# Constant ones for the warm-up, halves of W's first pieces on two engines, and V's and W's blocks in one load per step

## What is computed

```python
base = x @ W.T                                  # W 1024 x 1024
gates = top-2 softmax(x @ Wr.T + 5 * onehot(ids))
h = base + 2.0 * einsum('bter,bte,eor->bto', x @ A, gates, B)   # 8 experts, rank 16
hits = softmax(h @ cent.T / 0.1) > 0.01         # 64 clusters
query_sel, cluster_sel = hits.any(1), hits.any(0)
dense = h @ V.T + bias
out = x + where(query_sel & cluster_sel[assignments], dense, 0)
```

## Time and profile before

| | us |
|---|---|
| time, median of 3 | 334.21 (334.06 to 334.86) |
| the profiled execution's own time | 334.7 |
| its span | 332.9 |
| TensorE busy | 328.9 (99%) |
| VectorE busy | 263.0 (79%) |
| ScalarE busy | 137.2 (41%) |

### The profile page before, as it was taken

The page is one execution under the profiler, slowest core; times in us unless marked ns, Lnnn a source line. Parts: engine busy times, 40 slices in busy tenths (PEclk is TensorE's granted clock), DMA queues, the critical chain, the costliest instruction groups (busy, mean ns, idle before and its releaser), DMA issues.

```text
span 332.9 us, 4578 instructions
## 1 busy us (share of the span) xinstructions
PE 328.9 (99%) x1748; PEld 287.3 (86%) x1748; DVE 263.0 (79%) x477; ACT 137.2 (41%) x231; POOL 1.0 (0%) x9
## 2 busy tenths in 40 slices
PE   8999999999999999999999999999999999999996
PEld 5888889999999999999877888888888888888886
DVE  4837967168988998989996979679398594997995
ACT  4824645245755664765633313232223331331310
POOL 1000000000000000000000000000000000000000
PEclk9999999999999999999999999999999999999999
DMA  7965600333524433335712371805508237060113
GB/s 248 417 192 224 248 2 1 126 129 126 185 97 132 158 128 126 128 105 184 282 43 85 119 259 77 294 9 196 185 1 289 89 130 250 0 234 20 63 66 126
DMA packets 14070, 48.05 MB, mean 144 GB/s; under 512 B 1696, under 2 KB 1952, under 8 KB 14048
## 3 DMA queue, kind: packets, MB, share of 16 engines
q1 hardware_dynamic: 14048, 47.75, 40.5%
HBM read 39.36 MB, written 8.39 MB: 143 GB/s over the span
## 4 chain that ended last, share of the span: by engine, by line
PE 99%; DVE 0%; issue 0%
PE ps L1061 26%; PE ps L1062 26%; PE ps L1063 26%; PE ps L1142 8%; PE ps L1070 7%; PE ps L1144 4%; PE ps L1067 1%; PE ps L1155 1%; PE ps L1162 0%; PE ps L1164 0%; PE ps L1219 0%; DVE nat L1054 0%; DVE warm L694 0%; PE ps L1213 0%
## 5 line engine op out<-in xcount | busy, mean ns | idle before, releaser
L1061 PE MATMUL ps<-vt_hi,w_hi 128*128 128x288 f32 (+1 forms) x184 | 58.7, 319 | 0.0
L1063 PE MATMUL ps<-vt_hi,w_lo 128*128 128x288 f32 (+1 forms) x184 | 58.0, 315 | 0.0
L1062 PE MATMUL ps<-vt_lo,w_hi 128*128 128x288 f32 (+1 forms) x184 | 58.0, 315 | 0.0
L429 ACT ACTIVATE u<-ps 128x512 f32<-128x512 f32 x31 | 18.5, 597 | 80.9 <-PE ps L1063 54.2
L1062 PE MATMUL ps<-gop_lo,sl_s_hi 128*128 128x512 f32 x128 | 49.8, 389 | 0.0
L1142 PE MATMUL ps<-aw,xt_hi 128*128 128x400 f32 x128 | 38.9, 365 | 0.0
L1061 PE MATMUL ps<-gop_hi_t,sl_s_hi 128*128 128x512 f32 x96 | 37.4, 390 | 0.0
L1063 PE MATMUL ps<-gop_hi_t,sl_s_lo 128*128 128x512 f32 x96 | 37.3, 389 | 0.0
L1062 PEld LDWEIGHTS ps<-vt_lo,w_hi 128*128 128x128 f32 x184 | 34.6, 188 | 1.6
L1061 PEld LDWEIGHTS ps<-vt_hi,w_hi 128*128 128x128 f32 x184 | 34.5, 188 | 1.6
L1063 PEld LDWEIGHTS ps<-vt_hi,w_lo 128*128 128x128 f32 x184 | 34.5, 188 | 1.5
(11 more groups left out here) (144 smaller groups left out, 657.9 us busy)
## 6 DMA issues: line engine op xcount, KB each, us to landing
xt_raw<-in_xt SPq DMA_DIRECT2D x32, 512.0 KB, 3.9
nat<-in_x SPq DMA_DIRECT2D x16, 512.0 KB, 4.1
out<-nat SPq DMA_DIRECT2D x15, 512.0 KB, 2.7
w_raw<-in_w SPq DMA_DIRECT2D x7, 512.0 KB, 3.3
wraw<-in_w SPq DMA_DIRECT2D x5, 512.0 KB, 4.7
vt_raw<-in_v SPq DMA_DIRECT2D x4, 576.0 KB, 5.0
vt_raw<-in_v SPq DMA_DIRECT2D x4, 256.0 KB, 4.7
wq_raw<-in_wq SPq DMA_DIRECT2D x4, 256.0 KB, 4.8
```

The costliest lines, as they stand in the source:

```text
L429: return nc.scalar.activation(dst, src, ACT.Copy)
L1061: nc.tensor.matmul(dst, l_hi, r_hi, start=start, stop=False, skip_group_check=True)
L1062: nc.tensor.matmul(dst, l_hi, r_lo, start=False, stop=False, skip_group_check=True)
L1063: return nc.tensor.matmul(dst, l_lo, r_hi, start=False, stop=stop, skip_group_check=True)
```

## The change

- WARM_UP goes from 9 to 18, each warm-up matmul has 256 columns instead of 512, and both its operands are the framework's constant 1.0 in bfloat16, read with a step of zero, which GpSimd writes before the kernel's own instructions. The zeroed tile, its memset and its semaphore are gone.
- V's and W's pieces lie in one tensor vw in HBM and in one tile vw_raw in SBUF (128 x 8 x 2 x 512). Step 0's two pieces are still loaded one by one; from step 1 on one load brings both, with rows of 4 KB (one block) or 8 KB (two blocks). The tile lies in space that G uses later, and the lo parts no longer take the place of the raw values.
- In the steps 0 and 1 DVE copies W's columns 0 to 255 and ACT columns 256 to 511. TensorE waits for V's hi part and DVE's half, and for ACT's half ahead of the third block. From step 2 on ACT copies the whole of W's piece.
- Step 0 goes through the same loops as the others.
- The two halves of hit_sum are added by DVE, and TensorE counts them in one matmul.

```diff
-WARM_UP = 9
+WARM_UP = 18
...
+                if p == 0:
+                    sp.dma_start(vw_raw[:, 0, 0, :], piece(0, 1)).then_inc(v0_landed, 16)
+                    sp.dma_start(vw_raw[:, 0, 1, :], piece(1, 2)).then_inc(wq0_landed, 16)
+                else:
+                    sp.dma_start(vw_raw[:, j0:j1, :, :].rearrange("p k h f -> p (k h f)"),
+                                 piece(2 * j0, 2 * j1)).then_inc(vw_landed[p - 1], 16)
...
-                act.wait_ge(v1_landed[p], 16)
-                copy(vt1_hi[:, j, :], vt1_raw[:, j, :]).then_inc(v1_hi, 1)
-                act.wait_ge(wq_landed[p], 16)
-                copy(wq_hi[:, j, :], wq_raw[:, j, :]).then_inc(wq_hi_done, 1)
+                act.wait_ge(v0_landed if p == 0 else vw_landed[p - 1], 16)
+                copy(vt1_hi[:, j, :], vw_raw[:, j, 0, :]).then_inc(v1_hi, 1)
+                if p == 0:
+                    act.wait_ge(wq0_landed, 16)
+                cols = slice(2 * P, HALF) if p <= 1 else slice(0, HALF)
+                copy(wq_hi[:, j, cols], vw_raw[:, j, 1, cols]).then_inc(wq_hi_done, 1)
...
+                if p <= 1:
+                    dve.wait_ge(wq0_landed if p == 0 else vw_landed[0], 16)
+                    nc.vector.tensor_copy(wq_hi[:, j, 0:2 * P], vw_raw[:, j, 1, 0:2 * P]).then_inc(wq_half_hi, 1)
                 dve.wait_ge(v1_hi, p + 1)
...
-            nc.vector.memset(warm[:], 0.0).then_inc(warm_ready, 1)
...
-            nc.vector.tensor_copy(hit_b[:], hit_sum[:]).then_inc(hit_ready, 1)
+            nc.vector.tensor_tensor(hit_b[:], hit_sum[:, 0, :], hit_sum[:, 1, :], ALU.add).then_inc(hit_ready, 1)
...
-            pe.wait_ge(warm_ready, 1)
+            ones = nc.const_aps.tensor(1.0, [P, QUARTER], BF16)
             for _ in range(WARM_UP):
-                nc.tensor.matmul(ps[:, 0, :], warm[:, 0:P], warm[:], start=True, stop=True)
+                nc.tensor.matmul(ps[:, 0, 0:QUARTER], ones[:, 0:P], ones, start=True, stop=True)
...
+            for p in range(len(STEPS) - 1):
                 js = range(*STEPS[p])
                 pe.wait_ge(v1_hi, p + 1)
-                pe.wait_ge(wq_hi_done, p)
+                pe.wait_ge(wq_half_hi, min(p, 1) + 1)
                 for m in range(NQ):
+                    if m == (2 if p <= 1 else 0):
+                        pe.wait_ge(wq_hi_done, p + 1)
                     for j in js:
-                        first(m, wq_hi, j, vt1_hi)
+                        first(m, wq_hi, j, vt1_hi, start=j == 0)
```

More of the change, by code:

```diff
@@ L57, with adaln_ffn_kernel @@
 BANK_X, BANK_Y, BANK_V, BANK_W = range(4)
-def adaln_ffn_kernel(nc, x, xt, ids, w9, wq, awt, v1, v2, bias, assign, out):
+def adaln_ffn_kernel(nc, x, xt, ids, w9, vw, awt, v2, bias, assign, out):
     x_t = x.rearrange("b s d -> (b s) d")
@@ L90, in adaln_ffn_kernel @@
         hit_sum = sb("hit_sum", [P, 2, C], F32)
[L91 removed]
+        hit_b = sb("hit_b", [P, C], BF16)
         csel = sb("csel", [C, P], BF16)
@@ L117, in adaln_ffn_kernel @@
         hgt_all = sb("hgt_all", [P, NT * P], F32)
-        with nc.sbuf_tensor("warm", [P, HALF], BF16) as warm:
+        with nc.sbuf_tensor("vw_raw", [P, KO, 2, HALF], F32) as vw_raw:
             pass
@@ L184, in adaln_ffn_kernel @@
         ps_hgt = ps[:, BANK_HGT, 0:2 * P]
-        wq_landed = [sem(f"wq_landed{p}") for p in range(len(STEPS))]
-        wq0_hi = sem("wq0_hi")
+        wq0_landed = sem("wq0_landed")
+        wq_half_hi = sem("wq_half_hi")
         wq_hi_done = sem("wq_hi_done")
         wq_split = sem("wq_split")
-        v1_landed = [sem(f"v1_landed{p}") for p in range(len(STEPS))]
+        v0_landed = sem("v0_landed")
+        vw_landed = [sem(f"vw_landed{p}") for p in range(1, len(STEPS))]
         v2_landed = [sem(f"v2_landed{p}") for p in range(PIECES)]
@@ L328, in load_first, with piece @@
                 j0, j1 = STEPS[p]
[L329 to L335, removed]
+                def piece(a, b):
+                    return vw[0, a * P * HALF:b * P * HALF].rearrange("(q f) -> q f", q=P)
+                if p == 0:
[4 more added lines that the diff above has]
+                                 piece(2 * j0, 2 * j1)).then_inc(vw_landed[p - 1], 16)
             def load_v2(p):
@@ L462, in t_part @@
                 copy(gop_hi_t[:, :, jj, :], gop_raw[:, T1:T4 + 1, jj, :]).then_inc(t_hi, 1)
-            act.wait_ge(v1_landed[0], 16)
-            copy(vt1_hi[:, 0, :], vt1_raw[:, 0, :]).then_inc(v1_hi, 1)
-            for p in range(1, len(STEPS)):
+            for p in range(len(STEPS)):
                 split_first(p)
@@ L1211, in hit_counts @@
                 pe.wait_ge(hit_ready, 1)
-                for c in range(2):
-                    last = nc.tensor.matmul(ps[0:C, 7, 0:P], hit_b[:, c, :], ones_b[:], start=(c == 0), stop=(c == 1))
-                last.then_inc(count_ready, 1)
+                nc.tensor.matmul(ps[0:C, 7, 0:P], hit_b[:], ones_b[:], start=True, stop=True).then_inc(count_ready, 1)
             def column_mask():
@@ L1338, in both @@
         return [V[lo:hi], V[HALF + lo:HALF + hi]]
-    def in_steps(a):
-        return np.concatenate([a[:, j0:j1].reshape(1, -1) for j0, j1 in STEPS], 1)
-    v1 = in_steps(turned(np.concatenate(both(0, A1) + [cent], 0)).transpose(1, 0, 2).reshape(P, KO, HALF))
+    v1 = turned(np.concatenate(both(0, A1) + [cent], 0)).transpose(1, 0, 2).reshape(P, KO, 1, HALF)
     v2 = turned(np.concatenate(both(A1, A1 + A2) + both(A1 + A2, HALF), 0))
     w9 = np.concatenate([b, w], 0)
-    wq = in_steps(w9[0:NQ].reshape(NQ, P, KO, P).transpose(1, 2, 0, 3).reshape(P, KO, NQ * P))
-    return {"xt": xt, "w9": w9, "wq": wq, "awt": awt, "v1": v1, "v2": v2}
+    wq = w9[0:NQ].reshape(NQ, P, KO, P).transpose(1, 2, 0, 3).reshape(P, KO, 1, HALF)
+    vw = np.concatenate([v1, wq], 2)
+    pieces = [vw[:, 0, 0], vw[:, 0, 1]] + [vw[:, j0:j1] for j0, j1 in STEPS[1:]]
+    vw = np.concatenate([a.reshape(1, -1) for a in pieces], 1)
+    return {"xt": xt, "w9": w9, "vw": vw, "awt": awt, "v2": v2}
 def kernel(**inputs):
```

26 lines of the change are left out of this document (8 added, 18 removed).

## The result

The changed kernel takes 335.53 us (334.35 to 335.99, 11 runs) against 334.58 us (334.06 to 334.86, 11 runs) for the kernel before: 1.0026 of it, 95% interval 1.0016 to 1.0036. It is slower by 0.26%, where the forecast was 333.85 and a gain. The size is within what the text called hard to tell from no change, but eleven runs tell it, and it has the other sign and lies outside the range.

A forecast was written before the change was run, and what follows sets the result against it. TensorE, busy 99% of 332.9 us, was taken as the bound. An earlier step 1 gave 0.22 us, with hit counts 0.36, so 334.21 became 333.85; the range ran from 333.3 less 0.1 to 334.6.

The forecast's parts named there:

- Part 1, the warm-up: At the kernel's start, TensorE begins warm-up at about 0.80 us instead of 1.18, 0.38 earlier, without a wait.
- Part 2, the halves: W's step 0 copy split: DVE's half takes 0.29 us, ACT's 0.40; TensorE's first load at 4.52, 0.14 sooner.
- Part 3, one load per step: From step 1 on, V and W land together; step 1's weights are ready at 7.50 us instead of 7.72.
- The gate: Earliest start of TensorE's step 1 matmuls by its bytes: landing plus 0.95 us for wait, copy, semaphore and weights load.
- L: Landing time of step 1's double load, bounded by 6.14 and 6.77 us and taken as 6.55.
- the 8.2 which the forecast named as a sign of being wrong: Start of TensorE's step 1, expected at 7.4 to 7.7 or about 8.0 us; past 8.2 the forecast is wrong.
- Rival 4: Step 1's double piece lands late, at 7.4, so TensorE starts it at 8.35, 0.6 us worse: 334.7; chance 0.06.
- The sentence on coalescing: Skill's rule to join small transfers into one large; by it step 1 lands at or below 6.14, never gating.
- Part 4, hit counts: Near 173 us, one small TensorE matmul fewer saves 0.14 us (0.05 to 0.21); DVE's add costs nothing.
- The sum: Whole kernel, median run: 0.22 us from step 1's earlier start, with hit counts 0.36, giving 333.85 from 334.21.
- Rival 3: Hole of up to 0.2 us after warm-up makes TensorE's clock rise late, at 9.5 us: 336.3; chance 0.04.
- the median run as one in which the clock was up when the real work began: At TensorE's first real matmul, the median run of 334.21 us is assumed to pay no half-rate stretch, costing 0.45.

The follow-up runs named there:

- the two-load kernel: Changed kernel with V's and W's pieces of steps 1 to 3 loaded separately, steps 4 and 5 still double: 334.37 us against 334.44, ratio 0.9996.
- the trace with 7.69: Changed kernel, double loads kept, step 2's load held until V's step 0 piece landed, W's halves at step 0 alone: 334.35 us against 334.61, ratio 0.9992.
- the changed kernel's second trace: Changed kernel, nothing altered, measured once more in a later group against the kernel before: 335.13 us against 334.48, ratio 1.0014.
- held loads: Changed kernel, SyncE issuing step 2's load only once V's step 0 piece has landed: 334.60 us against 334.65, ratio 0.9999.
- The joint wait: Changed kernel with steps 1 to 3 in two loads, ScalarE and VectorE waiting for both pieces before copying either: ratio 0.9998 to the kernel before.
- the fastest kernel: Changed kernel with steps 1 to 3 in two loads and W's halves at step 0 alone: 334.14 us, ratio 0.9991; again 334.05, ratio 0.9984.

## Why the prediction was wrong

**Part 1, the warm-up: right.** TensorE's first instruction came at 0.77 (0.73 to 0.85 forecast), no wait is left. Alone it shortened the span by 0.26, of a size that its interval doesn't tell from nothing.

**Part 2, the halves: right in size.** 0.29 and 0.42 us against 0.29 and 0.40. The first real load began at 4.65, not 4.52, because W's step 0 piece landed at 4.24 in this execution and 4.12 in the other; counted from the landing it is 0.41 against 0.54 before. At step 1 the halves are not needed with two loads: without them the two-load kernel has a span of 332.41 and 332.34, with before's at 332.79 and 332.86. With double loads they are, as the trace with 7.69 shows.

**Part 3, one load per step: the step that failed.** The gate was L + 0.95, and that held to 0.14 us or better: in the changed kernel's second trace the copy starts at 7.44, the weights load at 8.12, and the first matmul takes the array at 8.23 by the spacings, and at 8.12 + 0.19 = 8.31 at the latest, against 7.42 + 0.95 = 8.37. That is past the 8.2 which the forecast named as a sign of being wrong. What failed is the bound on L, "by 6.14 (V's bytes alone) and 6.77 (both)". It was read off one execution of single loads, as if bytes in the same order landed at the same time however they are cut, and in every execution. Double loads with 4 KB rows land at 6.27 to 7.92, 0.6 us later than single ones on the mean of the traces, and even W's single piece came at up to 7.21, past the bound of 6.77. Rival 4 had the mechanism, at 7.4, with a chance of 0.06, and a price of 0.6; the kernel before with double loads alone measures 0.44 in the span. The sentence on coalescing, from the Trainium skill, "DMA: Bandwidth & Descriptors", "Rules for kernel authors", would have L at or below 6.14. None of the seven double loads with 4 KB rows landed that early (the earliest at 6.27); the one with 2 KB rows did, at 6.07. The trace agrees with the rule for the first eight of the 16 shares, which aren't later than those of a single load, and goes against it for the last ones. The rule is about throughput, and step 1 asks when the last byte of one piece is there.

**Part 4, hit counts: right in sign, under half in size.** From the product ahead of the counts to the one behind them it is 0.55 us before and 0.49 after, 0.06 less, against 0.14 (0.05 to 0.21):

```profile
172.63 0.39 PE L1063 MATMUL ps<-gb_hi,hgm_lo 128*128 128x512 f32 x1
...
173.18 0.50 PE L1061 MATMUL ps<-gop_hi_r,sl_s_hi 128*128 128x512 f32 x1
```

```profile
172.38 0.39 PE L1065 MATMUL ps<-gb_hi,hgm_lo 128*128 128x512 f32 x1
...
172.87 0.50 PE L1063 MATMUL ps<-gop_hi_r,sl_s_hi 128*128 128x512 f32 x1
```

That is about what 128 columns take (a quarter of the 0.227 for 512). The rest of the 0.43 that the forecast split between two matmuls stayed with the one. Over the whole kernel, from step 1 to the end, the two profiled executions differ by 0.02 only (324.73 and 324.71).

**The term that was not there.** The sum took the 1.8 us outside the span as fixed. It is 2.02 in the changed kernel, 0.22 of the 0.9 us lost, and goes with the two instructions by which VectorE's queue has grown (two waits and a copy more, a memset less). By the trace's counts no kernel is out of line: those with 563 or 564 have 1.79 to 1.81, those with 566 have 2.02 to 2.04, and the three with 567 have 2.12 or 2.13.

**The sum.** With L as bounded, the gain in the span was 0.36 by the forecast, and 0.35 with the loads in two. That these agree so closely is luck: the interval of that ratio is 0.3 us wide to either side, part 4 gave less than half of its 0.14, and with halves at step 0 alone the gain was 0.38 and 0.52. The double loads take it away and more (+0.19 to +0.9 in the spans of the five kernels with all loads double and nothing held), and 0.22 comes on top.

**Rivals.** Rival 3 (the clock rises late because of the hole) is out: filling the hole changed nothing (1.0024), and the new warm-up alone is no slower. The clock does vary between executions: with the old warm-up the first four real matmuls ran at 0.43 spacing, in the trace with held loads none (four of them within 1.16 us from 4.48). The forecast took the median run as one in which the clock was up when the real work began; by the spacings it was up in ten of the 20 traces and not in the other ten. Both kinds were forecast to gain, so the sign doesn't hang on it. The Trainium skill, "TensorE: Matmul & The Clock Gate", Part 1, has the point vary between runs of one kernel, and these traces agree. The clock accounts for spread, and in single traces for more than the loads do; the kernels with single and with double loads differ in the mean all the same.

**What stays open.** That the double loads cost the span is shown in both directions, by putting them into the kernel before and by taking them out of the changed one. Why their last shares come late is not. The joint wait is out. Two loads instead of one are no cure when the rows stay at 4 KB. The kernels with step 1 in two loads and with its 4 KB rows in two loads issue the same bytes in as many loads at nearly the same pace, and their spans are 0.12 shorter and 0.72 longer than before (0.44 without the one long run), which points at the length of the rows, or at the partitions that one load covers; but they were measured in different groups. Holding the next load back helps with the 4 KB rows kept. Whether the loads behind take the DMA engines from those ahead, or the last shares are late for another reason that queueing prolongs, no run separates. Held loads gained 0.27 in the span with W's halves in both steps and 0.19 with halves at step 0 alone, on two chips; two loads in steps 1 to 3 gained 0.33 to 0.52, so holding looks like the weaker cure, in part because W's copy then gates. Where the time outside the span lies, why it follows the number of VectorE's instructions, and what 565 or 568 would give, is open too.

## What to carry to other kernels

Loads at the start of a kernel are judged by when the last byte of the first pieces is there, not by their rate: here the pieces that TensorE met within a microsecond were better loaded one by one, while the later ones, of steps 4 and 5, stayed joined in the fastest kernel. Look at the last of a load's 16 shares, not at the mean. A bound on a landing time read from one trace is no bound; the spread between shares and executions belongs in the range. Find the one instruction whose start decides the rest of the span (here step 1's first matmul), and read every trace at that place. When kernels differ by 0.1%, compare spans and times apart, since even waits that never wait can move what lies outside the span, and count a queue's instructions in the trace, not in the source.

## What the runs showed of the hardware

- Three satisfied waits on VectorE, two instructions more by the trace, added 0.24 us outside the span (1.79 to 2.03), and taking two instructions away gave 0.22 back (2.02 to 1.80). Time outside by the number in VectorE's queue: 1.79 to 1.81 at 563 or 564, 2.02 to 2.04 at 566, 2.12 or 2.13 at 567.
- The 16 shares of one load can lie far apart: of a 512 KB load eight were there by 5.48 us and eight from 7.23 to 7.42.
- Between 4.0 and 4.5 us with loads queued the DMA engines moved 123 GB/s at a share of 0.57 in one execution, and 352 GB/s at 0.87 in another of nearly the same queue.
- Loads issued later can land the critical one sooner: step 1 at 6.26 and 6.42 with step 2 held, against 6.27 to 7.92 without.
- With nearly the same warm-up the clock was up ahead of the first real matmul in ten of 20 traces; in another the first four real matmuls still ran at 0.43 us each instead of 0.227.
